# Holding back each group's row gathers until the previous group's rows have landed, in a graph-attention kernel on Trainium2

## What is computed

```
Q, K, V = x @ Wq + bq,  x @ Wk + bk,  x @ Wv + bv        # per node, 8 heads of 12
E       = edge_attr @ We + be                             # per edge
score   = exp(clip(sum_over_12(K[src] * Q[dst] / sqrt(12) * E), -5, 5))
wV      = segment_sum(V[src] * score, dst);  Z = segment_sum(score, dst)
out     = layernorm(x + wV / (Z + 1e-6))
```

## Time and profile before

| | us |
|---|---|
| median of three runs (lowest, highest) | 1258.27 (1257.87, 1259.55) |
| the profiled execution's own time | 1255.49 |
| its span, first to last instruction | 1253.8 |
| PE matmul busy | 704.1 (56%) |
| POOL busy | 759.6 (61%) |
| DVE busy | 622.7 (50%) |
| ACT busy | 180.7 (14%) |

### The profile page before, as it was taken

How to read it: one execution, slowest core, us unless ns; L and a number is a source line. 1 busy time by engine, 2 the same in 40 slices (tenths; PEclk the granted TensorE clock), 3 DMA queues, 4 the chain that set the end, 5 groups by cost and what they waited for, 6 DMA issues and landing times.

```text
span 1253.8 us, 11903 instructions
## 1 busy us (share of the span) xinstructions
PE 704.1 (56%) x3376; PEld 478.2 (38%) x3376; DVE 622.7 (50%) x1205; ACT 180.7 (14%) x343; POOL 759.6 (61%) x788
## 2 busy tenths in 40 slices
PE   4573875665646455555654656655547464655554
PEld 3573543333334333333432434433334242333333
DVE  1221575555545455545554545544645364544546
ACT  1223211111101011111101111111111011111111
POOL 7262046665666666665665666665666666665660
PEclk8656896677777767777777676687767777687777
DMA  7373363553544454553553454453445464554440
GB/s 188 135 208 116 97 174 103 145 153 99 145 126 134 129 134 132 136 160 102 135 154 108 137 147 116 136 155 108 135 119 150 129 162 105 134 147 119 123 118 25
DMA packets 89940, 165.51 MB, mean 132 GB/s; under 512 B 43315, under 2 KB 61908, under 8 KB 86840
## 3 DMA queue, kind: packets, MB, share of 16 engines
q1 hardware_dynamic: 52843, 89.34, 25.7%
q0 software_dynamic: 37024, 75.35, 21.8%
HBM read 152.22 MB, written 12.39 MB: 131 GB/s over the span
## 4 chain that ended last, share of the span: by engine, by line
another core or an unknown queue 42%; PE 22%; issue 17%; DVE 11%; ACT 7%; DMA 1%; DVEq 0%; SPq 0%
PE psE L434 8%; ACT qe L601 6%; DVE qe L786 5%; PE psT L451 5%; PE psA L496 2%; DVE logit L875 2%; PE psQ L416 1%; PE psE L404 1%; DVE qke L866 1%; PE psA L461 1%; DVE msg L890 1%; DMA wn<-w_node 1%; DVE clipped L881 1%; PE psA L521 1%
## 5 line engine op out<-in xcount | busy, mean ns | idle before, releaser
L377 POOL DMA_INDIRECT kv<-kv_table,idx x750 | 727.9, 971 | 456.1 <-issue 218.6
L496 PE MATMUL psA<-place,msg 128*104 128x104 f32 x1564 | 205.0, 296 | 203.7 <-issue 159.6
L496 PEld LDWEIGHTS psA<-place,msg 128*104 128x104 f32 x1564 | 195.0, 209 | 230.2 <-issue 175.8
L434 PE MATMUL psE<-ea,we 97*96 97x512 f32 x392 | 267.8, 822 | 0.0
L451 PE MATMUL psT<-identity,qe 96*128 96x96 f32 x782 | 116.0, 309 | 213.1 <-DVE qe L786 185.4
L774 DVE TENSOR_TENSOR place<-psI,rel_tile 128x832 f32<-128x832 f32 (+1 forms) x99 | 98.5, 995 | 203.9 <-remote 189.0
L601 ACT ACTIVATE qe<-psE 96x1024 f32<-96x1024 f32 (+1 forms) x99 | 99.8, 1008 | 649.7 <-remote 496.5
L451 PEld LDWEIGHTS psT<-identity,qe 96*128 96x128 f32 x782 | 96.3, 181 | 227.6 <-DVE qe L786 192.3
L786 DVE TENSOR_TENSOR qe<-psQ,qe 96x1024 f32<-96x1024 f32 (+1 forms) x99 | 119.3, 1205 | 106.7 <-ACT qe L601 54.9
L866 DVE TENSOR_TENSOR qke<-psT,kv 128x768 f32<-128x768 f32 (+1 forms) x99 | 93.2, 942 | 151.4 <-remote 144.8
L434 PEld LDWEIGHTS psE<-ea,we 97*96 97x96 f32 x392 | 78.6, 226 | 84.2 <-issue 84.2
(11 more groups left out here) (107 smaller groups left out, 357.9 us busy)
## 6 DMA issues: line engine op xcount, KB each, us to landing
ea<-eaT SPq DMA_DIRECT2D x49, 768.0 KB
q_parts<-rel_table SPq DMA_DIRECT2D x24, 1008.0 KB
kv<-kv_table,idx POOLq DMA_INDIRECT x750
qwin<-q_table SPq DMA_DIRECT2D x198, 23.6 KB
xb<-xrows SPq DMA_DIRECT2D x24, 144.0 KB
out<-ob SPq DMA_DIRECT2D x24, 144.0 KB
q_table<-q_parts SPq DMA_DIRECT2D x4, 720.0 KB
kv_table<-kv SPq DMA_DIRECT2D x2, 960.0 KB
```

The source lines that it names most:

```text
L377: pool.indirect_dma_start(kv[:, k, t], None, kv_table, sources).then_inc(kv_in[k], 16)
L434: last = nc.tensor.matmul(psE[0:D, h, 0:size], we[:], ea[:, k // 2 % 2, edge:edge + size], start=True, stop=True)
L496: last = nc.tensor.matmul(psA[0:ML, off:off + PW], msg[:, s, t], place[:, s, t], start=opens, stop=closes)
```

## The change

Before the gathers of a group POOL now also waits for the landing of all the rows of the group in front of it. It concerns groups 8 to 98, in the pass that runs; `laps` is the number of times that slot `behind` has been filled by then (groups 0 to 3 did not fill theirs by a gather), and the last term allows for short groups.

```
@@ -369,6 +369,10 @@
                             pool.wait_ge(idx_rest_in, 16)
                             pool.wait_ge(kv_out, 16 * len(KV_CHUNKS))
                         k = at % U
+                        if first and at >= U:
+                            behind = (at - 1) % U
+                            laps = len(range(behind, at, U)) - (1 if behind < XG else 0)
+                            pool.wait_ge(kv_in[behind], 16 * (T * laps - (T - tiles(at - 1))))
                         for t in range(tiles(at)):
                             sources = bass.IndirectOffsetOnAxis(ap=idx[:, at * T + t:at * T + t + 1], axis=0)
                             if first and at < XG:
```

## The result

| | before | after |
|---|---|---|
| median, us (lowest to highest) | 1258.37 (1257.87 to 1259.55) | 1498.3 (1495.79 to 1500.12) |
| span of the profiled execution, us | 1253.8 | 1498.5 |
| granted clock of PE, mean | 0.735 | 0.709 |

The ratio of after to before is 1.1917, with a 95% interval of 1.1898 to 1.1937. The direction was right. The time lies outside the range of 1290 to 1450.

A forecast was written before the change was run, and what follows sets the result against it. POOL's gathers were taken as the bound, with a pause after every second group. Boundaries 310 instead of 164 us (+146) and the tail (-9) made 1255.5 into 1392.5 us, plus 2.8 for the median: 1395, range 1290 to 1450.

The forecast's parts named there:

- POOL as the bound, and its pause as what the change acts on: Groups 8 to 98: POOL's gathers set the time, with a pause after every second group; boundaries cost 164 us before.
- PE's pause for `q_done` is not added: At the group boundaries: the new wait covers the same us as the old pause, so nothing is added for it.
- rival 1: At the boundaries: PE's counts stay held, so POOL waits for `q_done` too; 81 us more, about 1476; 7%.
- A boundary is landing plus waking: At each of 90 boundaries POOL pauses for landing plus waking, 2.7 + 0.74 us, together 310 us.
- The waking: At a boundary: from the semaphore that let ACT go to POOL's start, about 0.74 us.
- The lag: From a group's last gather's end to its rows' landing: 2.7 us on average, 1.4 quiet, longer beside large loads.
- The eight gathers should still take 9.98 us: Within a group: POOL's eight gathers and seven steps keep their length, 7.77 + 2.21 = 9.98 us.
- The tail: After the last gather: a caught-up DVE finishes sooner, 9 us gained, 0 to 11 possible.
- Rival 2: At the gathers: shorter bursts free PE's counts and remove slow gathers, so not slower, 1255 us; 5%.
- Rival 3: At the boundaries: loads shift away from the groups' ends, all lags 1.35 us, mildly slower at 1273 us; 13%.
- The rule on queues: In the DMA engines: turns packet by packet would keep every lag near the quiet one; the prediction kept measured lags instead.

The follow-up runs named there:

- e13: Kernel before plus the new wait before even groups alone, where the kernel before took 1271.52 us: 1273.66 us, ratio 0.9998.
- e3: Kernel after with `ea` and `rel` loads shrunk to 64 columns behind the first two of each: 1293.26 us, ratio 1.2017 to the kernel before.
- e4: Kernel after with whole loads, SP holding an odd group's `ea` until the even group in front has landed: 1291.75 us, ratio 1.2000 to the kernel before.
- e5: Kernel before, unchanged, timed and traced again on the other kind of chip: 1080.75 us.
- e16: Kernel after with `ea` and `rel` issued only after the landing of the group under way, kernel before at 1271.52 us: 1339.9 us, ratio 1.0506.
- e11: Kernel after without DVE's `pick` instruction from group 9 on, its count kept: 1497.6 us, ratio 1.1737 to the kernel before.
- two_behind: Kernel after with the new wait asking for the rows of the group two in front: 1274.24 us against 1274.96 for the kernel before, ratio 0.9992.
- e10: Kernel before with `ea` and `rel` loads shrunk to 64 columns behind the first two of each: 1278.44 us, ratio 1.0016.
- e12: Kernel before without POOL's wait on `q_done`, on the slower kind of chip: 1323.1 us, ratio 1.0397.

## Why the direction was right and the size was not

**POOL as the bound, and its pause as what the change acts on:** right. POOL's pauses are 227 of the 251 us by which the stretch of the gathers grew, its slower gathers the other 24, and no other engine came to set the time.

**"PE's pause for `q_done` is not added".** Right, and shown by e13. After the change no long wait of POOL ends with "remote", so rival 1 did not happen. Its time, 1476, was the nearest of all to the 1498 measured, but for a wrong reason: that it came near is luck. Shorter bursts even let PE's counts come in time: before, ACT waited 496.5 us for `qe` with "remote" as the end, and after no wait for `qe` ends so. First before, then after:

```profile
ACT qe L601 <- remote: 496.5, 45, 13.9
```
```profile
ACT qe L605 <- PE psE L438: 251.4, 80, 6.4
```

**"A boundary is landing plus waking", 2.7 + 0.74.** This step failed, twice in the same direction, for 0.90 x 90 = 81 of the 108 us missed.
- *The waking.* 0.74 us was read from ACT's start to POOL's, so from the moment at which a count is there to that at which POOL works. (ACT and POOL wait there for two different semaphores, `e_done` and `q_done`, which the trace records as counted at 616.35 and 616.39; by the latter, POOL took 0.74 us.) As a waking it was right: it is 0.77 us in the kernel after. But the landing was read by the last packet, and between the last packet and the count lie 0.44 us, which neither term held. The two terms were measured at points that don't meet. From last packet to POOL's gather it is 1.21 instead of 0.74 us in the mean, 0.47 x 90 = 42 us. e3 and e4 confirm it: with nearly all lags quiet a boundary is 2.52 us, not 2.09.
- *The lag.* The pattern 6.6, 1.4, 3.5, 1.4 was in the prediction, with a mean of 3.2, and so was the reason why it would stay. Then it was weighed down to 2.7 with quiet stretches of the kernel before. Counted over all 90 boundaries that is what the kernel before has: a mean of 2.6 us, with a lag over 2 us behind 34 of the 45 even groups. The weighing carried this share over to a kernel in which the new wait locks the loads to the ends: there it is 43 of 45, the means of the four places are 6.1, 1.35, 3.7 and 1.37, and the mean of all is 3.13. The old pause is not what made the quiet stretches: e5, without it, has a mean of 2.4 and 25 of 45. 3.13 instead of 2.7 is 39 us. e16 puts the whole price of the meeting at 153 us.

**"The eight gathers should still take 9.98 us".** Wrong by +23.7 us. A full group takes 10.25 us in the kernel after, since the fourth gather of a group takes 1.34 us in the mean instead of 1.05. DVE now starts a group at nearly the same moment as POOL, so the same work of DVE falls on the same gather each time; that this work makes the gather slow is argued, not shown. For it speaks e5, where DVE too starts about 0.9 us after a landing: there a group takes 10.07 us without any change, with the sixth gather the slow one. Which of DVE's instructions it is stays open (without the pick most of it is still there, e11).

**The tail,** -9 us: right, -8.6 measured.

**The start:** group 8 begins 2.6 us later; the step was not in the prediction.

The sum of what was missed: 42 + 39 + 23.7 + 2.6 + 0.4 (the tail) = 107.7, and 244.7 - 137 = 107.7 us. The profiled execution's own time was 1500.12 us, and the median this time lies 1.8 below it, where 2.8 us above were put on top; that makes the 103 us between 1395 and 1498.3.

**Rival 2** (the break pays) was right that PE's counts come in time with short bursts, and wrong that this buys anything: arithmetic was never short of time here. **Rival 3**, all lags quiet, is what e16 built by hand: its profiled execution took 1342.65 us, where 1270.5 had been reckoned for the first chip. Its boundaries sum up to 233 us instead of the 188 reckoned (+45, of which 36 are the unseen part between packet and count), its gathers take the 24 us more of the kernel after too, and group 8 starts 3 us later.

**The rule on queues.** The prediction took a sentence of the Trainium skill ("DMA: Bandwidth & Descriptors", Queues, rings and completion order), that a DMA engine takes turns between queues packet by packet, as one packet of a gather for one of a load. By that reading each lag would have been near the quiet one; 6.4 us for the last 96 packets of a group beside `ea` and `rel`, against 1.35 us without them, exclude that. They don't exclude what the section says: its packet is a bundle of typically 9 to 17 descriptors, and no run here shows how that bundle relates to what the profile counts as packets.

## What to carry to other kernels

Before a wait for a landing is put in front of the queue that bounds a kernel, add up everything from the issuer's last instruction to its next one, measured at one and the same place (last packet, visible count, restart): here 2.4 us at best and 7.6 with the two large loads beside it, for each time that the queue runs empty. Asked one group later the wait cost nothing here, as `two_behind` shows. And if a regular pattern of collisions is found, reckon with a wait at every step locking it in, as it did here, before averaging it with stretches in which it is absent.

## What the runs showed of the hardware

- The same kernel takes 1077 and 1081 us on two chips and 1258 to 1275 us in the jobs on others. In the slower ones PE's counts are seen late while POOL issues gathers without a break: at 600 to 640 us some 2 us after the last gather of a burst of sixteen. The counts themselves are recorded so late: PE's last query product before that ends at 605.3 us, and `q_done` is counted at 616.39. With bursts of eight, in the kernel after, it does not happen (POOL: no "remote"; boundaries 390.6 and 391.5 us on the two kinds of chip). Neither the loads (e10) nor the wait for `q_done` (e12) is the cause, which stays open. A version that is best on both kinds of chip wasn't found: without the `q_done` wait it is 2.3% faster on one and 4.0% slower on the other.
- In the quiet groups of the kernel after it takes 1.35 us from the end of the last gather's issue to its last packet, about 0.4 us more to the last count of the semaphore, and 0.77 us from the count to POOL's next gather. DVE, waiting for the same semaphore, starts 0.09 us after the count. (The last three are medians of all 90 boundaries.)
- Loads of 768 and 1008 KB on another queue, issued while a group's last gathers run, stretch those 1.35 us to about 6.4; the 768 KB alone to about 3.7.
